# Softmax attention: the value products of two key tiles as one block in TensorE's step, the output copy at the head of ScalarE's step

## The reference

```python
    q, k, v = (proj(Wq), proj(Wk), proj(Wv))
    cos, sin = _rope_cos_sin(S, dk)
    q, k = _apply_rope(q, k, cos, sin)
    scores = jnp.einsum('bhqd,bhkd->bhqk', q, k) / jnp.sqrt(jnp.float32(dk))
    attn = jax.nn.softmax(scores, axis=-1)
    out = jnp.einsum('bhqk,bhkd->bhqd', attn, v)
    out = out.transpose(0, 2, 1, 3).reshape(B, S, D)
    return out @ Wo.T
```

## Time and profile before

| what | value |
|---|---|
| time, median of 3 runs | 2611.47 us (2608.74 to 2611.81) |
| the profiled execution | 2616.47 us, span 2614.8 us |
| granted TensorE clock, mean over the span | 0.962 of full speed |
| the stage of the change, first maximum product to last value product | 241.8 to 1107.0 us |
| busy share of the span | PE 93%, DVE 65%, ACT 50%, POOL 44% |

### The profile page before, as it was taken

How to read it: one execution, slowest core, us unless ns; L and a number is a source line. 1 busy time by engine, 2 the same in 40 slices (tenths; PEclk the granted TensorE clock), 3 DMA queues, 4 the chain that set the end, 5 groups by cost and what they waited for, 6 DMA issues and landing times. The chain is left out here.

```text
span 2614.8 us, 47880 instructions
## 1 busy us (share of the span) xinstructions
PE 2426.8 (93%) x14630; PEld 1345.7 (51%) x14630; DVE 1710.8 (65%) x3843; ACT 1300.4 (50%) x2634; POOL 1156.4 (44%) x1436
## 2 busy tenths in 40 slices
PE   7997899999999999879899996899999969898998
PEld 4663133333333333356556774566666646556776
DVE  6777788888888888369533323688888759733322
ACT  4664576767766776634322332455555424322322
POOL 6999111110111111033226775677777723225676
PEclk9998799999999999989998998999999989998999
DMA  5655433333333231046757984011111026775886
GB/s 174 206 196 164 104 94 92 91 93 89 95 87 101 81 102 56 29 157 198 238 176 201 229 192 74 15 38 37 37 38 34 22 81 204 231 214 160 218 212 113
DMA packets 290884, 325.10 MB, mean 124 GB/s; under 512 B 30481, under 2 KB 272289, under 8 KB 290721
## 3 DMA queue, kind: packets, MB, share of 16 engines
q1 hardware_dynamic: 257024, 274.22, 34.8%
q0 software_dynamic: 29184, 46.43, 8.9%
q10 hardware_dynamic: 4512, 2.40, 0.4%
HBM read 217.23 MB, written 105.19 MB: 123 GB/s over the span
## 5 line engine op out<-in xcount | busy, mean ns | idle before, releaser
L714 DVE TENSOR_REDUCE a_row_max<-a_ps_m 128x2 f32<-128x1024 f32 x512 | 607.6, 1220 | 83.6 <-PE a_ps_m L612 78.7
L763 ACT ACTIVATE a_probs<-a_ps_s 128x512 f32<-128x512 f32 x1024 | 536.9, 601 | 234.5 <-PE a_ps_s L639 234.2
L654 PE MATMUL a_ps_o<-a_probs,a_va 128*32 128x512 f32 x2048 | 274.1, 608 | 0.8 <-ACT a_o_sb L772 0.8
L1681 POOL TENSOR_TENSOR b_spread<-b_decay,held_own_sb 128x512 f32<-128x512 f32 x256 | 269.3, 1085 | 8.2 <-DVE b_weight L1742 8.2
L1742 DVE TENSOR_TENSOR b_weight<-b_ps_s,b_spread 128x512 f32<-128x512 f32 x256 | 163.8, 682 | 17.6 <-PE b_ps_s L1882 17.6
L639 PE MATMUL a_ps_s<-first_qs,first_ks 98*128 98x512 bf16 (+1 forms) x512 | 161.0, 396 | 6.9 <-DMA first_qs<-a_m_parts 6.9
L639 PE MATMUL a_ps_s<-second 98*128 98x512 bf16 (+1 forms) x512 | 156.7, 386 | 5.1 <-DMA second<-a_m_parts 3.1
L547 POOL CAST a_high<-a_row_max 128x32 bf16<-128x32 f32 x32 | 6.6, 206 | 322.5 <-DVE a_row_max L714 322.3
L588 POOL DMA_DIRECT2D x<-a_xo x32 | 24.2, 757 | 274.6 <-DVE a_xo L748 272.2
L315 PE MATMUL a_ps_qk<-a_w_qk,a_xnT 128*128 128x512 f32 x256 | 122.2, 600 | 0.0
L612 PE MATMUL a_ps_m<-first_ks,first_qs 48*128 48x512 bf16 x512 | 106.6, 414 | 10.6 <-DVE a_row_max L714 9.3
(11 more groups left out here) (383 smaller groups left out, 5556.9 us busy)
## 6 DMA issues: line engine op xcount, KB each, us to landing
parts<-second SPq DMA_DIRECT2D x16, 1536.0 KB, 6.2
second<-parts SPq DMA_DIRECT2D x384, 64.0 KB, 2.3
rows<-m_early SPq DMA_DIRECT2D x32, 640.0 KB, 3.2
m_early<-x SPq DMA_DIRECT2D x32, 512.0 KB, 4.0
first_qs<-parts SPq DMA_DIRECT2D x192, 64.0 KB, 2.4
first_ks<-parts SPq DMA_DIRECT2D x192, 64.0 KB, 2.2
m_own<-in_L_ffn_w_gate_dram SPq DMA_DIRECT2D x24, 384.0 KB, 4.4
m_own<-in_L_ffn_w_up_dram SPq DMA_DIRECT2D x24, 384.0 KB, 5.7
```

The lines of the kernel that those rows point to most:

```text
L654: last = nc.tensor.matmul(ps_o[VW * j:VW * (j + 1), :], va[n.u][:, t, (h0 + j) * VW:(h0 + j + 1) * VW], probs[:, group % 2, j, t, :], star ...
L714: nc.vector.tensor_reduce(row_max[:, n.k // 4 % 2, t, :, n.p % 4], m_bank(name, step)[:], AX.X, ALU.max).then_inc(m_drained, 1)
L763: nc.scalar.activation(probs[:, group % 2, j, t, :], s_bank(name, step)[:], ACT.Exp, scale=DK ** -0.5).then_inc(s_drained, 1)
L1681: nc.gpsimd.tensor_tensor(spread[:, n % 2, heads].rearrange("p h t c -> p (h t) c"), decay[:, n % 3, heads].rearrange("p h (t o) -> p (h t ...
```

## The change

On PE both value blocks of a pair stand together, with lag 7, behind scores 2 and 3. The turned output and the turned shift are now neighbours, with no value block between or before them. On ACT the output copy comes ahead of exponential 0. Counts, shapes, buffers and the turns of the buffers are as before.

```diff
-            walk_pairs(pe, [(0, max_products(0)), (L_S, scores(0)), (L_S, scores(1)), (L_OTURN, turn_output), (L_MIX + 1, mix_values(1)),
-                            (L_TURN, turn_shift), (0, max_products(1)), (L_S, scores(2)), (L_S, scores(3)), (0, max_products(2)), (L_S, scores(4)), (L_S, scores(5)), (L_MIX, mix_values(0)),
-                            (0, max_products(3)), (L_S, scores(6)), (L_S, scores(7)),
+            walk_pairs(pe, [(0, max_products(0)), (L_S, scores(0)), (L_S, scores(1)), (L_OTURN, turn_output), (L_TURN, turn_shift),
+                            (0, max_products(1)), (L_S, scores(2)), (L_S, scores(3)), (L_MIX, mix_values(0)), (L_MIX, mix_values(1)),
+                            (0, max_products(2)), (L_S, scores(4)), (L_S, scores(5)), (0, max_products(3)), (L_S, scores(6)), (L_S, scores(7)),
                             (L_ATT[0], turn_att(0)), (L_ATT[1], turn_att(1)), (L_OUT[0], project(0)), (L_OUT[1], project(1))])
-            walk_pairs(act, [(L_S, exponentials(0)), (L_S, exponentials(1)), (L_OCOPY, copy_output)]
-                       + [(L_S, exponentials(i)) for i in range(2, 8)] + [(L_ATT[0], copy_att(0)), (L_ATT[1], copy_att(1))])
+            walk_pairs(act, [(L_OCOPY, copy_output)] + [(L_S, exponentials(i)) for i in range(8)] + [(L_ATT[0], copy_att(0)), (L_ATT[1], copy_att(1))])
```

## The result

| | before | changed |
|---|---|---|
| median | 2610.1 us (4 runs) | 2677.86 us (2670.65 to 2680.36, 4 runs) |
| ratio | 1 | 1.0252, 95% interval 1.0233 to 1.0271 |
| span of the profiled execution | 2614.8 us | 2675.0 us |
| last value product starts | 1107.0 us | 1174.4 us |
| the rest of the span behind it (untouched code) | 1507.8 us | 1500.6 us |

The change makes the kernel 2.5% slower: +67.8 us between the medians, where +64 was forecast (2675 against 2677.86). The whole of it stands in the stage that was changed. Its end comes 67.4 us later; the code behind it took 7 us less in this execution. That part, the same in all ten kernels profiled here, took between 1497 and 1510 us, so 7 us of it is no finding.

What follows compares the result with a forecast made beforehand. PE was taken to bound the stage. Waits of +83 us, less 3 of old waits and 18 of saved starts, gave +62; with +2 at the stage's end, 2611.5 + 64 = 2675 us, range 2640 to 2722.

Steps and rivals of the forecast that it cites:

- What bounds the stage: PE bounds the stage, busy 51.59 of 51.85 us in a period of 8 steps, with 0.19 us of waits.
- The saved start: On PE a further value block in a row costs 0.855 us, not 1.00: 0.145 saved a step, 1.16 a period.
- The two buffers: On PE maximum products wait for the two `ps_m` buffers DVE drains: 0.26 us in a plain step, 0.81 with a turned output.
- the output step behind a projection: Twice a period PE waits 0.58 us until DVE, late from the projection's residual, has reduced maximum 0.
- POOL's chain: Turned shift waits for POOL's split of the maxima, taken as 1.2 us: PE waits 1.41, or 0.88 behind a turned attention.
- The copy: ACT's output copy, moved ahead of exponential 0, costs nothing; a block no longer waiting for it gains nothing.
- The sum: Over the stage +4.16 us a period, 15 periods, gives +62; with +2 at its end, 2611.5 + 64 = 2675.
- The end of the stage: In the last five steps, without maxima, ACT starves during a double block: +2 us.
- nothing exposed: Rival: in the stage `ps_m` waits stay under the double block and only saved starts count: -17 us, 2594; chance 3%.
- only the shift exposed: Rival: of PE's waits in the stage only those at the turned shift appear: +14 us, 2626; chance 7%.
- The clock's rival: Rival: PE's clock also falls to the lower level in each of the 30 shift steps: +50 us, 2725; chance 15%.
- a falling clock in the stage: Sign of a wrong mechanism: the stage's granted clock falls, where 1.00 was forecast.

Runs made afterwards that it cites:

- shorter reductions: Changed kernel, and the kernel before as control, both with DVE's row maxima over 256 of 512 keys: 2608.3 us, control 2606.93 us.
- blocks one pair apart: Changed kernel with the second value block moved behind scores 4 and 5, so two single blocks: 2661.1 us, ratio 1.0198 to the kernel before.
- the blocks alone: Changed kernel with ACT's part undone: value blocks joined on PE, output copy behind exponential 1 as before: 2680.97 us, ratio 1.0267 to the kernel before.
- the turned output and shift behind scores 3: Changed kernel with both moved from behind scores 1 to just ahead of the double block, buffer turns and DVE's order moved along: 2646.54 us, ratio 1.0128.
- the kernel without POOL's chain: Changed kernel in which the turned shift takes POOL's split of the maxima from the group before, with more buffers: 2658.43 us, ratio 1.0189.

## Why the prediction was right

| kind of step | by hand | measured | how many in 8 |
|---|---|---|---|
| plain | 5.55 | 5.56 | 1 |
| plain behind a turned attention | 6.00 | 6.05 | 1 |
| with a turned output | 6.69 | 6.69 | 2 |
| output behind a projection | 8.30 | 8.34 and 8.43 to 8.54 | 2 |
| with a turned shift | 7.24 | 7.25 | 1 |
| shift behind a turned attention | 7.24 | 7.25 | 1 |
| period | 56.0 | 56.3 | |

- *What bounds the stage*: right. PE did, with 0.2 us of waits in a period; the change put 5.9 there (56.37 less 51.66 - 1.16), where 5.5 were forecast. The profile shows 4.4 of them as idle time, 8% of the period where the prediction said 10%, because the modelled ends of products reach into the waits.
- *The saved start*: right in size, 1.85 for a double block. By the sum it is worth some 17 us, against waits of 5 times that.
- *The two buffers*: right, shown by the shorter reductions and by the blocks one pair apart. The mis-sized term is the output step behind a projection: 0.63 and 0.72 to 0.83 of waits in place of 0.58. There the projection's group itself takes 2.00 us in place of 1.89, and the turned output often starts 0.08 later, which my hand-following left out. A turned attention takes 0.59 (532.32 to 532.91), not the 0.53 that was taken, hence 6.05 in place of 6.00. And in a plain step the 0.26 is not DVE's alone: with short reductions ACT's pace holds PE there for nearly as long.
- *POOL's chain*: right (1.2 assumed, shift at 4.01 against 3.99), though the profile's label names POOL only behind a turned attention.
- *The copy*: right, free with the moved blocks. I gave no price for it without them; it is 54 us between the medians.
- *The sum*: from the second turned shift to the last, 15 periods, the profiled stage takes 844.35 us in place of 773.50. Of these +70.9 the three falls of the clock are 4.5, so 66.4 stand against the forecast's 62. The end of the stage, put at +2 for ACT, is 2.7 us shorter instead (34.5 in place of 37.2 from the last shift to the last block, which now has lag 7 in place of 8), and 0.8 us was gained ahead of all this: 67.4. So the sum came within 4 us partly by luck: the longer steps and the falls, which it left out of the forecast, were half made up by an end that it had with the wrong sign.
- *The rivals*: nothing exposed, and only the shift exposed, are both out. The clock's rival came true in a small part, 3 of 30 shift steps in place of all. The prediction called a falling clock in the stage a sign of a wrong mechanism; these three falls are 4.5 us of 67 and don't make it one. Over the ten kernels the clock fell six times between its first rise and the last maximum product (three here, one with the blocks alone, two with the turned output and shift behind scores 3), each time behind an idle time of PE of 1.11 to 1.29 us. There were 32 idle times of that size, so most passed without a fall; the 16 of 1.01 to 1.09 us in the kernel with one pair apart all did.
  The page "TensorE: Matmul & The Clock Gate" of the Trainium skill (section "A second HAM failure mode: psum-queue depth-cycling") puts such swings down to small idle times between groups of bf16 products. Here groups with idle times of 0.5 us did not bring them (75 in the kernel without POOL's chain, and no fall), and an idle time of more than 1.1 us did, at times. What decides between one such step and the next stays open.

## What to carry to other kernels

A block of work of one kind that stands between two users of a small ring of buffers is not only work: it is the time in which the ring is drained. Before joining such blocks, follow one step by hand from the durations of the trace, with each buffer's release and each chain of another engine that the block covered, once for every kind of step. It took six numbers here, and gave each kind of step within 0.3 us.

## What the runs showed of the hardware

- Going over to another kind of product costs PE about 0.15 us for a value block (1.00 alone, 0.855 each in a row) and about 0.1 for a maximum product (0.32 alone, 0.54 for two). What in the change of kind costs this (shape, type, place in the array) no run takes apart.
- The granted clock can fall to 0.53 inside a stage whose PE is busy 92% of the time, behind one idle time of 1.1 to 1.2 us; 13 of 16 such steps of the changed kernel pass without it.
- In all ten kernels the stage begins at a granted clock of 0.50, with maximum products and later scores but no value block yet, and the clock rises to 1.00 only 1.0 to 4.4 us after the start of the first value block (before: 291.25 and 294.2 us). In the kernel before PE had no idle time from 276 to 290 us, and the clock stayed at 0.50. Whether the value block is the cause was not tried.
